# TensorE's weighing product of a unit placed between the scores of its two pairs of banks

## The reference

```python
# layer 0, per head; causal
att = softmax(mask(q1 @ k1.T / sqrt(8))) - lam * softmax(mask(q2 @ k2.T / sqrt(8)))
y = head_norm(att @ v) * (1 - LAMBDA_INIT);  s = y @ c_w
# layer 1, per head; the last 128 keys, keys before the sequence score 0 and have no value
s = (softmax(scores / sqrt(8)) @ v) @ wo.T + bo
# both
x = x + s * silu(experts(xn))
```

## Time and profile before

| | us |
|---|---|
| runs | 1578.10, 1582.63, 1588.72 |
| median | 1582.63 |
| the profiled execution | 1578.77 |
| its span, first to last instruction | 1577.0 |
| PE busy | 1091.8 (69%) |
| DVE busy | 814.3 (52%) |
| ACT busy | 783.4 (50%) |
| POOL busy | 541.3 (34%) |

### The profile page before, as it was taken

How to read it: one execution, slowest core, us unless ns; L and a number is a source line. 1 busy time by engine, 2 the same in 40 slices (tenths; PEclk the granted TensorE clock), 3 DMA queues, 4 the chain that set the end, 5 groups by cost and what they waited for, 6 DMA issues and landing times. The chain is left out here.

```text
span 1577.0 us, 38797 instructions
## 1 busy us (share of the span) xinstructions
PE 1091.8 (69%) x12282; PEld 812.3 (52%) x12282; DVE 814.3 (52%) x1742; ACT 783.4 (50%) x1828; POOL 541.3 (34%) x851
## 2 busy tenths in 40 slices
PE   1400699858888888888886150079985778778886
PEld 1400699835555555555553140069983555555554
DVE  5411466546776677677641441245644555555550
ACT  2170356515677677777665111036551556555654
POOL 2276100001255445545545207610000243344344
PEclk9999999957999999999988555589995898888887
DMA  6051122222232223222300005122221222212211
GB/s 173 13 180 47 57 69 69 57 60 70 49 80 66 52 49 86 59 51 66 75 15 8 0 2 167 47 61 68 67 57 41 56 57 58 53 51 61 56 42 28
DMA packets 166104, 95.59 MB, mean 61 GB/s; under 512 B 18546, under 2 KB 159748, under 8 KB 165956
## 3 DMA queue, kind: packets, MB, share of 16 engines
q1 hardware_dynamic: 157764, 76.82, 18.5%
q0 software_dynamic: 8192, 16.79, 3.6%
HBM read 30.19 MB, written 24.64 MB: 35 GB/s over the span
## 5 line engine op out<-in xcount | busy, mean ns | idle before, releaser
L1331 DVE TENSOR_REDUCE at_maxima<-ps 128x2 f32<-128x512 f32 (+1 forms) x576 | 374.7, 686 | 271.7 <-PE ps L1024 243.0
L1220 ACT ACTIVATE at_probs<-ps 128x512 f32<-128x512 f32 x576 | 323.2, 597 | 132.6 <-PE ps L1024 113.8
L1023 PE MATMUL ps<-tables 64*128 64x256 bf16 (+1 forms) x2304 | 235.4, 265 | 155.7 <-DMA stack<-at_pieces 51.4
L616 ACT ACTIVATE ex_hid<-ps,ex_w 128x128 f32<-128x128 f32 x576 | 164.9, 369 | 262.7 <-PE ps L586 262.5
L1024 PE MATMUL ps<-stack 62*128 62x256 bf16 (+3 forms) x3072 | 271.9, 259 | 1.5 <-issue 1.5
L1023 PEld LDWEIGHTS ps<-tables 64*128 64x128 bf16 x2304 | 94.9, 97 | 264.8 <-issue 231.9
L578 PE MATMUL ps<-ident,ex_rows 128*128 128x128 f32 x144 | 40.4, 281 | 206.6 <-DMA ex_rows<-list_in 206.3
L1024 PEld LDWEIGHTS ps<-stack 62*128 62x128 bf16 (+1 forms) x3072 | 170.9, 101 | 14.1 <-issue 2.0
L656 DVE COPY ex_w<-ex_weights 128x1156 f32 x144 | 109.9, 763 | 111.6 <-issue 111.6
L523 POOL DMA_INDIRECT list_in<-ex_rows,ex_slots x128 | 124.6, 973 | 112.6 <-DVE ex_slots L629 69.8
L586 PE MATMUL ps<-ex_rowsT,ex_w 128*128 128x128 f32 x1152 | 157.7, 281 | 1.3 <-DVE ex_rowsT L649 1.3
(11 more groups left out here) (171 smaller groups left out, 1483.6 us busy)
## 6 DMA issues: line engine op xcount, KB each, us to landing
stack<-at_pieces SPq DMA_DIRECT2D x192, 128.0 KB
stack<-at_pieces SPq DMA_DIRECT2D x192, 64.0 KB
ex_rows<-list_in SPq DMA_DIRECT2D x144, 64.0 KB, 1.8
list_out<-ex_result SPq DMA_DIRECT2D x144, 64.0 KB, 1.5
list_in<-zero_tile SPq DMA_DIRECT2D x1, 4608.0 KB, 17.7
ex_weights<-in_L_w SPq DMA_DIRECT2D x4, 1024.0 KB
ex_weights<-in_L_w SPq DMA_DIRECT2D x16, 256.0 KB
x<-in_L_attn_x SPq DMA_DIRECT2D x4, 512.0 KB, 6.0
```

What stands on the lines that cost most here:

```text
L616: last = nc.scalar.activation(hid[q % 2][:, hb, :], hid_ps[q % 2][:, hb * P:(hb + 1) * P], gelu, bias=w[q][:, B1 + hb:B1 + hb + 1])
L1023: return nc.tensor.matmul(fine(bank, j), R.eye[tile, j, :], mask[tile], start=(j == 0), stop=True, skip_group_check=(j > 0))
L1220: nc.scalar.activation(probs[:, (n // 3) % 2, n % 3, i * 512:(i + 1) * 512], t_bank[i], ACT.Exp, scale=SCALE).then_inc(t_free, 1)
L1331: nc.vector.tensor_reduce(by_half[:, h0:h0 + heads, a], s_bank[i].rearrange("p (m k) -> p m k", k=P * (late + 1)), AX.X, ALU.max).then_inc ...
```

## The change

In PE's queue the weighing product of a unit is moved ahead of the scores of the unit's second pair of banks. Nothing else is changed: the same instructions, waits and buffers.

```diff
--- before.py
+++ after.py
@@ -1173,12 +1173,12 @@
                 par = r % 2
                 for n in range(UNITS):
 
-                    for i in range(2):
-                        both_scores(step, r, n, i)
+                    both_scores(step, r, n, 0)
                     if n < 2 and has(step, "last"):
                         weigh(step - 1, 1 - par, GROUPS - 1, n)
                     if has(step, "now") and n >= 3 and n % 3 < 2:
                         weigh(step, par, n // 3 - 1, n % 3)
+                    both_scores(step, r, n, 1)
                     for name in NAMES:
                         if has(step, name) and n == SLOT[name]:
                             general_use(step, r, name)
```

## The result

The changed kernel took 1590.65 us (median of 20 runs, 1581.47 to 1607.18) and the kernel before 1578.44 us on the same chip (20 runs, 1571.42 to 1591.13). The ratio is 1.0078, with a 95% interval of 1.0053 to 1.0103: 12.3 us slower (8.4 to 16.3). The forecast was 10 us slower. The profiled execution after took 1588.49 us, with a span of 1586.7 us, 9.7 us longer than before.

What follows compares the result with a forecast made beforehand. PE nearly bounds layer 0, a ring of waits through all engines sets layer 1's step. Layer 0's +1.5 and layer 1's +8.4 make +10 us: 1582.63 + 10 = 1592 us, range 1574 to 1610 for 8 in 10.

Steps and rivals of the forecast that it cites:

- layer 1's term: Layer 1: ACT does one bank more behind the release, 0.6 us x 14 = +8.4 us; bounds 0 and +20.
- layer 0's: Layer 0: PE's gains nearly cancel ACT's lateness, +0.1 us a step, +1.5 us in all; bounds -9 and +7.
- The wait moves ahead and is no new one: PE, units with n % 3 = 0: product waits for ACT's second bank of the unit before, as pair 1 must anyway.
- the 0.62 us that PE could gain at most: Layer 0, each step: pair 1's excess waits go, 0.18 in unit 10, 0.2 in unit 0, 0.24 in unit 1.
- the 0.5 us that were to arrive at unit 0: Layer 0: ACT loses 0.65 us between unit 9's banks, recovers 0.16, so unit 0 begins about 0.5 us later.
- The release behind the gathers: Layer 1: PE creeps while POOL gathers, until about 1479.3; unit 4's pair 1 would come out only then.
- the mean of +0.6 us a step: Layer 1: ACT's extra bank, 0.60 us, before copy, gate and the probabilities unit 0 waits for, in each of 14 steps.
- If pair 1 slips through ahead of the gathers: Layer 1's lower bound: pair 1 of unit 4 gets through before the gathers, and the cost is 0.
- that sign of the prediction: Layer 1: unit 0's wait for ACT, 2.13 us before, should grow.
- Only the stalls go: Rival: PE loses layer 0's pair 1 excess, ACT catches up, layer 1's moved bank hides; -9 us, 1574; chance 0.25.
- The transfers set layer 1: Rival: DVE's later split delays layer 1's transfers, 1.4 us a step counting in full, +20 us; 1604; chance 0.16.
- The clock: Rival: closer packing keeps PE's clock up behind layer 1's release, saving half of 5.57 us a step, 39 us; 1544; chance 0.04.

Runs made afterwards that it cites:

- the late divide: Kernel before, PE order unchanged, with layer 1's DVE divide put behind the last split in unit 5 instead of in unit 4: 1591.83 us, ratio 1.0023 (0.9996 to 1.0050).

## Why the prediction was right, point by point

**The sum** was +10 us and came out at +12.3. It holds because layer 1's term was right in size (+7.9 where +8.4 stood) and layer 0's, small in the forecast, was mis-sized by 5 us (+6.5 where +1.5 stood; the interval, 2.5 to 10.6 us, takes in its upper bound of +7, but not the +1.5). That the time itself came so near, 1590.65 us where 1592 stood, is partly luck: the base of three runs lay 4.2 us above that of twenty. And the size of layer 1's term was right by a way that the rows do not bear out, as said below.

**PE itself.** The pairs stand a product apart and the short stalls of pair 1 are gone, as forecast. "The wait moves ahead and is no new one" holds: in unit 9 it is 1.58 us ahead of pair 1 before and 1.52 us ahead of the product after, 18.5 and 15.9 us in fifteen steps. What was left out is the next unit: pair 1 of unit 5 now waits until unit 4's late bank is read (8.4 us), which the wait for the transfers covers. Of the 0.62 us that PE could gain at most, unit 10 brought 0.14 and units 0 and 1 next to nothing (from one unit's pair 0 to the next unit's, means of ten steps: 2.39 to 2.25, 2.46 to 2.49 and 2.89 to 2.83 us). The regular steps lost nothing: 30.39 and 30.47 us with all units moved, just under all ten kernels with the old order, about as small a change as was drawn, and on the side of a gain; a difference of 0.2 us is near the spread of single profiles.

**ACT in layer 0.** The idle time between the two banks is there in unit 10 (0.33 us), not in unit 9, and unit 0 did not wait longer for ACT (0.35 us in the step shown; 0.68 in the earlier trace rows). So the 0.5 us that were to arrive at unit 0 did not (the loss in unit 9 was 0.6 by its own terms, 483.1 - 482.5, not 0.65). What failed is the count of 14 equal steps. The loss is not in the regular ones: the last three steps cost 3 to 6 us more, where PE, at the lower clock, is busy and ACT waits for its second banks; the fifth step shows another 1 to 3.5 us in the three kernels in which units 3 to 10 were moved, the least of them within the spread of the other ten.

**Layer 1, unit 4.** This carries the cost, as forecast: +7.7 us with that unit alone, nothing with the others that this measurement tells. The release behind the gathers is in the rows too. But the mean of +0.6 us a step hid an alternation: long steps near 24.5 us and short ones near 20.5, as the gathers begin with unit 4 or some 0.9 us behind it. "If pair 1 slips through ahead of the gathers" was given as a bound for all steps; it is every second step. And the way to the next step was drawn through ACT, for which unit 0 waits; there the wait halved (15.7 to 7.0 us), so that sign of the prediction failed. The rows show another way: DVE's search of the late bank, then pair 1 of unit 5, which has waited up to 3.8 us in one piece, and then rows of PE at the lower clock; PE's waits in all are no longer than before. That this chain is the price was read from rows; no kernel changed it alone. Nor is it the whole price, since the move costs something without the gathers too.

**The rivals.** Only the stalls go: wrong, both layers lose. The transfers set layer 1: with the gathers in place the last split ends 10.50 us behind the first search of unit 3 before and 10.38 after (means of eleven steps), so they start no later, and this rival's 20 us did not come; the late divide gained nothing either. Without the gathers PE waits for them in each step. The clock: 0.93 and 0.84 against 0.92 and 0.84, so packing closer gave nothing back; its 39 us were set too high as well, since the like stretch of layer 0 takes 3.33 us (487.00 to 490.33), which is not half of 5.57. The prediction had the clock only as a gain; over twelve steps of layer 1 it looks like a loss, 0.82 to 0.85 in the three kernels with unit 4 moved against 0.85 to 0.86 in five without, and that term was not in the sum. The Trainium skill's rule in "TensorE: Matmul & The Clock Gate", section "A second HAM failure mode: psum-queue depth-cycling", that short gaps between groups of matmuls can unsettle the clock, had no effect that these rows show: the short gaps ahead of pair 1 closed, and the clock rose by no more than 0.01.

**Open:** what the move costs beyond the later split when the gathers are gone; whether the lower clock is the price in layer 1 or goes along with it; and why PE regains its clock later at the end of layer 0.

## What to carry to other kernels

Putting a long product between two banks' producers gives the producer fewer stalls and hands each reader of the second bank a delay of the product's length, in every unit; ask which reader has no slack, and ask it again for the first and last steps, where other engines have run out of work. When a bank comes late, follow it past its first reader to whoever needs the bank back: here that was the producer itself, one unit on, in both layers. When a wait seems new, look for it under another name before the change: a trace puts a wait for two engines down to one of them. When the waits are no longer and the time is, compare the engine's busy time for the same work. Before multiplying a per-step price by the number of steps, look at two neighbouring steps; here they took turns.

## What the runs showed of the hardware

In the steps shown, what waits for PE while POOL issues its four gathers gets its banks late, though PE's matmul rows stand before: in layer 1 the pair's rows begin at 1369.74, ACT begins at 1374.64, and the last gather's row ends at 1373.39; in layer 0 the rows end at 478.38 and ACT begins at 480.38, with gathers from 476.10 to 480.91. It is not so all through the gathers: in the next step of layer 1 a bank arrives at 1394.14, 1.07 us after they began, right behind its rows. Leaving out layer 1's gathers, 64 transfers, took 31 us off the kernel, on an engine that is busy 34% of the span. Whether PE itself, its signals or its instruction supply are held up is not told apart by these runs. After PE had idled 3.79 us behind such a late bank, its next 3.81 us ran at a granted clock of 0.51.
